# Lower attention masks kept in the adjacency, fillers for TensorE at five joints, and the last feature groups moved behind the preparation's flag

## The reference

```python
def _gat_conv(x, src, dst, W, a_src, a_dst, b, n_nodes):
    h = x @ W.T
    alpha_s = h @ a_src
    alpha_d = h @ a_dst
    e = _leaky(alpha_s[src] + alpha_d[dst], NEG_SLOPE_ATT)      # slope 0.2
    m = jax.ops.segment_max(e, dst, num_segments=n_nodes)
    ex = jnp.exp(e - m[dst])
    z = jax.ops.segment_sum(ex, dst, num_segments=n_nodes)
    return jax.ops.segment_sum(h[src] * (ex / z[dst])[:, None], dst, num_segments=n_nodes) + b
...
src = jnp.concatenate([edge_index[0], loops])                    # every node also points to itself
dst = jnp.concatenate([edge_index[1], loops])
h = _leaky(_graph_norm(_gat_conv(x, ..., W1, ...)), 0.01)
h = _graph_norm(_gat_conv(h, ..., W2, ...))
return _leaky(h + residual, 0.01)
```

## Time and profile before

| what | us |
|---|---|
| median of three runs | 830.65 |
| profiled execution, whole | 833.16 |
| its span, first to last instruction | 830.9 |
| matrix built | 0 to 194 |
| two graph convolutions | 194 to about 317 |
| two mean aggregations | to 455 |
| first preparation | 455 to 486 |
| first attention, PE's products | 488.7 to 604.5 |
| graph norm and second preparation | 604.5 to 636 |
| second attention, PE's products | 638.7 to 754.4 |
| last norm and last aggregation | to 831 |

### The profile page before, as it was taken

One profiled execution on the slowest core, in us unless ns is written; L12 is line 12 of the kernel. 1 busy time (PEld: TensorE's weight loads), 2 busy tenths in 40 slices (PEclk: granted clock), 3 DMA queues, 4 the chain that ended last, 5 costly groups with the idle time before them and its releaser, 6 DMA issues. The chain is left out here.

```text
span 830.9 us, 20752 instructions
## 1 busy us (share of the span) xinstructions
PE 735.1 (88%) x8249; PEld 673.3 (81%) x8249; DVE 614.3 (74%) x1462; ACT 467.9 (56%) x911; POOL 4.8 (1%) x15
## 2 busy tenths in 40 slices
PE   7888888887997999999999749999963999997997
PEld 6655555556996999999999649999862999897997
DVE  7999999996447445533444579999978899996742
ACT  2888898882004123222133669988665898883600
POOL 2000000000000000000000000000000000000000
PEclk9899999998997999999999559999965999998999
DMA  4000000002992000000000210000001299977901
GB/s 140 13 11 13 13 5 1 2 2 81 418 417 95 2 2 2 2 2 2 2 25 13 84 34 17 18 17 2 2 1 34 43 204 202 196 160 156 202 26 35
DMA packets 98732, 56.00 MB, mean 67 GB/s; under 512 B 91160, under 2 KB 93130, under 8 KB 98504
## 3 DMA queue, kind: packets, MB, share of 16 engines
q1 hardware_dynamic: 98288, 53.77, 24.2%
q10 hardware_dynamic: 344, 0.85, 0.3%
...
## 5 line engine op out<-in xcount | busy, mean ns | idle before, releaser
L656 PE MATMUL banks<-y_sb,adjacency 128*128 128x192 f16 (+1 forms) x1875 | 166.9, 249 | 4.6 <-DVE y_sb L696 3.9
L1810 PE MATMUL banks<-x_sb,gat_masks 128*128 128x194 f16 x880 | 157.7, 252 | 14.8 <-DVE gat_masks L1731 12.0
L656 PEld LDWEIGHTS banks<-y_sb,adjacency 128*128 128x128 f16 x1875 | 162.1, 99 | 5.6 <-DVE y_sb L696 4.0
L1781 ACT ACTIVATE gat_masks<-y_sb,node_scalars 128x640 bf16<-128x640 f32 x176 | 133.4, 821 | 20.4 <-PE banks L1811 15.8
L486 PEld LDWEIGHTS counts<-hot_code,hot_row 128*128 128x128 f16 x1568 | 88.4, 98 | 67.9 <-DVE hot_code L361 42.4
L486 PE MATMUL counts<-hot_code,hot_row 128*128 128x100 f16 (+3 forms) x1568 | 121.4, 214 | 23.5 <-DVE hot_code L361 17.5
L1811 PE MATMUL banks<-loose,gat_masks 128*128 128x194 f16 x790 | 141.2, 251 | 0.0
L1810 PEld LDWEIGHTS banks<-x_sb,gat_masks 128*128 128x128 f16 x880 | 87.7, 100 | 18.7 <-DVE gat_masks L1724 13.6
L361 DVE TENSOR_TENSOR hot_code<-codes_iota,unpacked 128x600 f16<-128x600 f16 x196 | 97.0, 557 | 0.0
L597 ACT ACTIVATE adjacency<-counts 128x800 f16<-128x800 f32 x98 | 81.6, 833 | 17.9 <-PE counts L486 17.8
L1724 DVE TENSOR_TENSOR gat_masks<-gat_masks,adjacency 128x1280 f16<-128x1280 bf16 (+1 forms) x94 | 72.9, 778 | 11.3 <-ACT gat_masks L1781 10.6
...
...
## 6 DMA issues: line engine op xcount, KB each, us to landing
...
residual<-h_sb SPq DMA_DIRECT2D x5, 240.0 KB, 2.0
...
loose<-residual SPq DMA_DIRECT2D x5, 240.0 KB, 3.5
x_sb<-kept_x SPq DMA_DIRECT2D x5, 240.0 KB, 4.6
x_sb<-in_x SPq DMA_DIRECT2D x4, 240.0 KB
```

What stands on the lines that cost most here:

```text
L656: return nc.tensor.matmul(k.ps[:, j % G, 0:cols], k.ADJ[:, i, j * P:(j + 1) * P], y[:, i, 0:cols], start=i == 0, stop=i == NT - 1)
L1781: nc.scalar.activation(step_of(x), row[ch % 2], ACT.Relu, bias=k.a_s5[:, i:i + 1], scale=STEEP).then_inc(t.step_ready, 1)
L1810: nc.tensor.matmul(bank[:, 0:2 * BC], mask_of(over_slots, x)[:, q * P:(q + 1) * P], features[0][:, i, :], start=i == 0, stop=False)
```

## The change

It has four parts.

**Lower masks in place, units of three.** `under` writes counts minus upper mask over the counts in `k.ADJ` itself, and PE reads the lower mask there. Lower masks need no slots any more. A unit is now one or three steps (`MOST_TILES = 3`): the first chunk has 4 single ones and 7 triples, the other four 1 and 8. `OWN` is 4 slots of three steps. The first attention therefore destroys the matrix, and SP brings it back: `reload_chunk` loads a chunk of 640 columns from `kept_adj` in five transfers, waits for the one with the diagonal blocks and loads those, with self loops, from `kept_diagonal`, which the first preparation stores. Four chunks are reloaded during the first attention once PE has used them (`used`), the fifth in the second preparation, ahead of the destination values' round trip. In the second attention DVE waits for a chunk's reload, and the transposed loads wait for PE's `used` instead of DVE's `under_ready`. `write` adds both halves in one instruction, and `DRAINED` is later.

**Features behind the flag.** `low(2)` and `scaled(3)` are done where `low(3)` and `scaled(4)` stood, and `low(3)`, `scaled(4)`, `low(4)` with ACT's `high(3)` and `high(4)` follow in the attention's block, ahead of DVE's read of the flag. PE waits for them (`low_ready`).

**Sizes from PSUM.** The last group's `largest` reads the products in PSUM, and does not wait for ACT's copy of them. That copy and the exponentials of the last group come later on ACT.

**Fillers.** PE gets `keep_busy` products of 128 columns: 10 and 10 at the end of the matrix's build, 10 and 8 at the start of the first convolution, five runs of 8 to 16 while its batch norm is computed, in the first preparation 14 + 12 + 12 + 12 ahead of the first product, 6 behind each group's product and 12 at the end, and 32 at the start of each attention. The second preparation gets none.

```diff
-BUSY_FIRST, BUSY_NEXT = 60, 45
+BUSY_FIRST, BUSY_NEXT, BUSY_TAIL = 60, 45, 10
...
         last.then_inc(degree_ready, 1)
+        stay_busy(BUSY_TAIL)
         pe.wait_ge(out_deg_ready, 1)
         nc.tensor.matmul(total_ps, ...).then_inc(total_ready, 1)
+        stay_busy(BUSY_TAIL)
...
+        keep_busy(nc, k, 7, 10)
+        pe.wait_ge(s.high, 1)
+        keep_busy(nc, k, 7, 8)
         pe_aggregate(k, nc, pe, s, k.Y, s.y_ready, 2, ONE + 1, turn)
...
+        keep_busy(nc, k, 4, 10)
+        for event, count, times in ((s.measured, NC + 1, 10), (s.var_h, 1, 8), (s.dev_h, 1, 10), (s.affine, 1, 16)):
+            pe.wait_ge(event, count)
+            keep_busy(nc, k, 4, times)
...
     def largest(dve, g):
+        source = tiles(k.Hg, g) if g < NG - 1 else products(g)
+        if g < NG - 1:
+            dve.wait_ge(s.emptied_a, g + 1)
...
         if first:
+            sp.wait_ge(s.looped, 2)
+            for from_tile, end, blocks in diagonal(k, 0, NT):
+                sp.dma_start(d.kept_diagonal[:, from_tile:end, :], blocks).then_inc(s.diagonal_kept, 16)
+        else:
+            reload_chunk(k, d, sp, NG - 1)
         sp.wait_ge(s.ad_copied, 1)
         sp.dma_start(d.a_dst, HT[0][0:NT, 0:P]).then_inc(s.ad_stored, 16)
...
-        low(NG - 2)
-        scaled(NG - 1)
+        low(dve, NG - 3)
         chain.later(dve.tensor_scalar(k.a_s5[:, :], k.a_s[:, :], STEEP, None, ALU.mult))
...
-        low(NG - 1)
+        scaled(dve, NG - 2)
...
+    def last_features(dve):
+        low(dve, NG - 2)
+        scaled(dve, NG - 1)
+        low(dve, NG - 1)
+
+    def last_highs(act):
+        high(act, NG - 2)
+        high(act, NG - 1)
...
+            if g == 1 and first:
+                busy_until(7, (k.x_added, NT, 14), (k.h_ready, NT - 4, 12), (k.h_ready, NT - 2, 12), (k.h_ready, NT, 12))
             if g >= 1:
                 multiply(g - 1)
+                if first:
+                    keep_busy(nc, k, 7, 6)
+        if first:
+            busy_until(7, (s.copied, NG, 12))
...
-OWN, UNBRANCHED = 7, 2
-MOST_TILES = 2
-SINGLES = (3, 1, 1, 1, 1)
+OWN, UNBRANCHED = 4, 2
+MOST_TILES = 3
+SINGLES = (4, 1, 1, 1, 1)
-DRAINED = (4, 5, 7, 8, 9)
+DRAINED = (6, 6, 8, 9, 11)
...
+def reload_chunk(k, d, sp, m):
+
+    for n, a in enumerate([m] + [a for a in range(NG) if a != m]):
+        sp.dma_start(k.ADJ[:, a * G:(a + 1) * G, m * G * P:(m + 1) * G * P],
+                     d.kept_adj[a * G * P:(a + 1) * G * P, m * G * P:(m + 1) * G * P]
+                     .rearrange("(t p) q -> p t q", p=P)).then_inc(k.adj_first if n == 0 else k.adj_back[m], 16)
+    sp.wait_ge(k.adj_first, 16 * (m + 1))
+    for first, end, blocks in diagonal(k, m * G, (m + 1) * G):
+        sp.dma_start(blocks, d.kept_diagonal[:, first:end, :]).then_inc(k.adj_back[m], 16)
...
             def under(u):
                 dve.wait_ge(t.over_ready, u + 1)
-                if under_slots[u][1]:
-                    dve.wait_ge(t.used, under_slots[u][1])
-                dve.tensor_tensor(masks(under_slots, u, F16), counts_of(u), masks(over_slots, u, F16),
-                                  ALU.subtract).then_inc(t.under_ready, 1)
+                dve.tensor_tensor(counts_of(u), counts_of(u), masks(u, F16), ALU.subtract).then_inc(t.under_ready, 1)
...
+            keep_busy(nc, k, 1, 32)
+            pe.wait_ge(k.low_ready, 2 * NG)
             for ch in range(NG):
...
         @block.vector
         def _(dve):
+            k.last_features(dve)
             wide = dve.value_load(k.wide[0:1, 0:1], min_val=0, max_val=1)
...
         @block.scalar
         def _(act):
+            k.last_highs(act)
             for x in range(UNBRANCHED):
                 step(act, x)
```

170 lines of the change are left out of this document (103 added, 67 removed).

## The result

| | before | changed |
|---|---|---|
| median of the runs, us | 830.65 (830.48 to 831.51, 3 runs) | 820.02 (818.57 to 820.42, 3 runs) |
| ratio, 95% interval | | 0.9865 [0.9843, 0.9887] |
| profiled execution: whole, span, us | 833.16, 830.9 | 818.57, 816.8 |

The change gains 10.6 us; 15.9 were forecast. The two profiled executions lie 14.6 us apart. That of before was a long one for its kernel (31 later runs of that kernel, in three sets, have medians of 831.3 to 831.4 and lie between 829.2 and 834.0), that of the changed kernel the shortest of its three. So the trace is used for where time went, and the medians for how much.

What follows compares the result with a forecast made beforehand. PE was taken as bound by half clock behind idle stretches, the attentions by DVE's masks and PE closely together. Terms 2.0 + 2.0 + 2.5 - 0.4 + 9.8 = 15.9 us off 830.65 gave 814.7 us, range 807 to 827.

Steps and rivals of the forecast that it cites:

- A: Build's end and first convolution: fillers keep PE at full clock there; 2.0 us gained, bounds 0 to 2.5.
- C: First preparation's loop: fillers bring PE to full clock, last group taken out earlier; 2.5 us gained.
- D: Last group taken out to PE's first attention product, twice: features moved behind the flag; 0.4 us worse for both.
- B: Batch norm: 54 fillers give full clock in the last transposes and second convolution's start; 2.0 us gained.
- E: Both attentions: triple masks, fewer PE waits and a shorter start; 4.9 us gained each, 9.8 for both.
- rival 1: The clock falls in PE's gaps despite fillers, so most gains shrink; 3.4 us gained, 827.2 us; chance 0.18.
- Rival 3: Attentions: PE's 4.5 us of waits stay, each gains 2.0 by its start only; 820.5 us; chance 0.12.
- Rival 2: PE is at full clock at once, every gain at its upper bound; 22.5 us gained, 808.2 us; chance 0.17.
- Rival 5: The change does nothing: fillers never move the clock, PE alone sets the attention's pace; 830 us; chance 0.03.
- Rival 4: Second preparation: the reload delays the destination values' round trip, first step 57 us late; 872 us; chance 0.05.

Runs made afterwards that it cites:

- e2: The changed kernel without any of the added fillers; 825.01 us, ratio to the kernel before 0.9923.
- e4: The changed kernel without the 54 fillers of the batch norm alone; 819.44 us, ratio to the kernel before 0.9869.
- e7: The changed kernel with 8 more fillers behind each group of batch norm transposes, 12 behind the last; 819.11 us, ratio to the kernel before 0.9851.
- e9: The changed kernel with the last two groups' low and high parts put back ahead of the flag, both preparations; 820.67 us, ratio to before 0.9878.
- e1: The changed kernel with no edit, timed again beside the kernel before; 820.63 us, ratio to before 0.9873.
- e8: The changed kernel with fillers in the second preparation too; 819.63 us, ratio to the kernel before 0.9859.
- e10: The changed kernel with the sums of a chunk taken in the kernel before's earlier steps (`DRAINED`); 841.37 us, ratio to before 1.0123.
- e11: The changed kernel with DVE making lower masks first in units 3 to 9, and dividing sums behind a lower mask in later chunks; 814.22 us, ratio 0.9795.
- e6: The changed kernel with in-place masks in units of two steps instead of three; 820.07 us, ratio to the kernel before 0.9864.
- e3: The kernel before plus all the added fillers, nothing else of the change; 823.92 us, ratio to before 0.9916.

## Why the prediction was right in direction and 5 us off

The direction held, and so did the mechanisms of A, C and D; B failed, and E gained less than forecast and in part for another reason. The sum was 5.3 us too high, and the time lies inside the forecast's range of 807 to 827. Terms below are the forecast's, sizes from the two tables.

**A (2.0, bounds 0 to 2.5): about 1.5.** The twelve traces with these fillers have 61.52 us eight times and 62.5 to 63.2 four times, 61.95 on average; without them 63.92 and 62.94. The execution that I read had the long stretch at half clock; the filler-free kernel of e2 had a short one. The term was sized from one execution, and the average over executions is smaller.

**B (2.0): nothing.** This is the step that failed. I let 54 fillers ahead of the first transposes hold the clock through 6 us in which PE is busy little more than half the time. The trace shows the fall at 259.8, among the transposes, with waits of 0.4 to 0.6 us between them; e4 shows that the fillers can be left out, and e7 that fillers among the transposes hold it, with 2.2 us to gain (201.1 against 203.3 on average). Against "the others lie beside ACT": they do, and that leaves PE too idle.
The forecast set beside rival 1 the Trainium skill, "TensorE: Matmul & The Clock Gate", section "HAM oscillation", by which a burst followed by a wait makes the next burst cold. Of that the trace shows the end and not the cause: the second convolution began at 0.50, but behind a stretch of short waits, the longest 1.0 us, and not behind one long one. Rival 1's own price for B, 1.0, was nearer to the measured nothing than the forecast's 2.0. In C it did not bite, 11.34 to 11.64 us at a clock that falls, at the earliest, in the last group.

**C (2.5): 3.5 to 3.8.** The full-clock sum of the forecast (472.5, 11.2 us behind the first product) was nearly exact, and so was its mechanism, PE's pace for three groups and DVE's 3.0 us for the last two; the discount for a clock that might fall was not needed. In the changed kernel the groups are taken out at 460.2, 462.2, 464.1, 467.1 and 470.4; the third and fourth as rows:

```profile
464.12 0.16 DVE L1300 COPY node_scalars<-banks 128x5 f32<-128x5 f32 x1
...
467.13 0.15 DVE L1300 COPY node_scalars<-banks 128x5 f32<-128x5 f32 x1
```

**D (-0.4 both): -0.4.** The size was right (12.54 and 12.34 against 12.27 and 12.25), and so were both sides of its sum: the flag's end comes 5.6 us behind the last group instead of 9.1, 3.4 earlier, and PE's first product 6.9 behind the flag instead of 3.2, 3.7 later. With the order of before, in e9, the first lower mask comes 0.1 us later, 0.3 in the second attention; the stretch itself is 2.0 and 2.8 us longer there by the fillers, and that is given back in the attention.

**E (9.8): 7.9 in the first pair of traces, 6.4 against e1's.** Of its two parts the rest was nearly exact and the start too short. The rest of an attention was forecast at 103.5 and 1.5 of waits, 105.0; it is 104.8. The start was forecast at 5.9 us for 40 products with a low clock; from the first product to the 41st it took 6.9 in the first attention at a full clock, 7.1 in the second with the clock low for its first 2.8 us, and 7.6 in e1 at a low one, because DVE's order keeps the fourth single unit's lower mask behind a wait for ACT. Seven traces have this order at the first attention's start: 6.9 us in the three at 1.00 (e4 and e8 too), 7.6 in the four at 0.50 (e1, e2, e7, e10). The clock is worth 0.7 us there, the order 2.0 (e11). First to last product that makes 111.6 us in the first attention, against 110.9 forecast and 115.8 before. The waits behind the start are 1.7 us where 1.5 was forecast, yet my reason for them to go, the pace of the masks, was wrong: with doubles in place they go as well (e6). That the size fits is in part luck. The forecast's second reason, more steps in slots, is not parted by any run from the later sums, which it took for a cost. Triples at 1.08 us (517.56 to 518.63 below) and the in-place mask at no cost were right.

```profile
517.56 1.16 DVE L1814 TENSOR_TENSOR adjacency<-adjacency,gat_masks 128x1920 f16<-128x1920 f16 x1
518.63 1.16 DVE L1810 TENSOR_TENSOR y_sb<-y_sb,adjacency 128x1920 f16<-128x1920 bf16 x1
```

With these sizes: 1.5 + 0 + 3.6 - 0.4 + 7.2 (mean of the two traces) = 11.9, against 10.7 by the medians, whose interval is 8.8 to 12.3. Of the 4.0 us between this and the forecast, E has 2.6, B 2.0 and A 0.5, and C gives 1.1 back.

**The rivals.** Rival 3's number, 820.5, is the time measured, and its mechanism is not: the waits went (4.5 us missing before, 1.8 now), each attention gained 3.2 to 4.0 and not 2.0, and the difference was made up by B. It also called the later sums a cost; e10 shows the opposite. Rival 1's low clock came in B, in some executions of A and at some starts of the first attention. Rival 2's full clock came in C, and at the first attention's start in three of the seven traces, where the order kept PE waiting all the same. Rival 5 is out by e2 and e3. Rival 4 is out by the reload's own rates, which answer; its queue entry, and the window in which it lands:

```profile
599.44 4.45 SPq L1504 DMA_DIRECT2D adjacency<-kept_adj  x5
...
617.65 0.32 SPq L1285 DMA_DIRECT2D a_dst_rows<-y_sb  x1
```

```profile
605.00:606.00 1.00, 1.00 (x7) 1.00 (x6) 1.00 (x2) 0.98 (x2) 0.00 (x0) 0.50 1.07 362
```

4.1 MB at 362 GB/s is over by 613, 4 us ahead of the row's store. Whether the round trip could have overtaken it, no run shows. The section that the forecast names for it, the Trainium skill, "DMA: Bandwidth & Descriptors", "Queues, rings and completion order", gives the order in which descriptors are taken, and adds that a later one may finish its write before an earlier one.
